# Moving the output stores and input loads of a cross-attention kernel to other steps of a tile

## What is computed

```python
q = heads(x @ W_q)
k_t, v_t = heads(text @ W_k), heads(text @ W_v)
probs_t = softmax(einsum('bhsd,bhtd->bhst', q, k_t) * attn_scale)
text_out = einsum('bhst,bhtd->bhsd', probs_t, v_t)
attn_scores = einsum('bhsd,bhnd->bhsn', q, k_ip) * attn_scale
qsem = l2norm(einsum('bhst,bte->bhse', probs_t, text))
fused = attn_scores + 0.5 * einsum('bhse,bne->bhsn', qsem, l2norm(ip))
probs_ip = softmax(fused) * spatial_mask
out = (text_out + probs_ip @ v_ip) @ W_out + b_out + x
```

## Time and profile before

| what | value |
|---|---|
| median of 3 runs | 1042.71 us (1041.78 to 1043.53) |
| time of the profiled execution | 1040.03 us |
| its span, first to last instruction | 1038.2 us |
| TensorE matmul busy | 981.1 us, 95% |
| VectorE / ScalarE / GpSimd busy | 78% / 68% / 62% |
| the DMA queue's packets, share of 16 engines | 84.3% |
| mean granted TensorE clock | 0.982 |

### The profile page before, as it was taken

The page is one execution under the profiler, slowest core; times in us unless marked ns, Lnnn a source line. Parts: engine busy times, 40 slices in busy tenths (PEclk is TensorE's granted clock), DMA queues, the critical chain, the costliest instruction groups (busy, mean ns, idle before and its releaser), DMA issues.

```text
span 1038.2 us, 24562 instructions
## 1 busy us (share of the span) xinstructions
PE 981.1 (95%) x7604; PEld 791.6 (76%) x7604; DVE 806.9 (78%) x2401; ACT 707.7 (68%) x2315; POOL 641.9 (62%) x1899
## 2 busy tenths in 40 slices
PE   7986778999999999999999999999999999999877
PEld 5755666888877888888877888888878888888755
DVE  4375678888978788888878888888868888887851
ACT  1354778777677777777766777777767787777720
POOL 1112467777676677667666767767756677676750
PEclk9988999999999999999999999999999999999989
DMA  9845988979799998888899989798889989679852
GB/s 292 325 129 133 192 160 157 165 169 186 160 191 178 186 190 172 172 169 169 156 200 180 186 172 182 156 187 167 164 179 193 177 172 184 138 158 150 161 116 74
DMA packets 483871, 180.26 MB, mean 174 GB/s; under 512 B 449517, under 2 KB 461855, under 8 KB 483740
## 3 DMA queue, kind: packets, MB, share of 16 engines
q1 hardware_dynamic: 483708, 178.62, 84.3%
q10 hardware_dynamic: 32, 0.07, 0.0%
HBM read 42.34 MB, written 27.22 MB: 67 GB/s over the span
## 4 chain that ended last, share of the span: by engine, by line
PE 76%; DMA 5%; DVE 3%; ACT 2%; SPq 2%; issue 2%; POOL 1%; POOLq 0%; DVEq 0%; ACTq 0%
PE ps_O L1149 25%; PE ps_Q L1183 25%; PE ps_S L1122 12%; PE ps_U L1169 11%; DMA pts<-ph 5%; PE ps_M L1199 3%; ACT pr L905 2%; SPq L825 1%; SPq L795 0%; ACT ph L917 0%; DVE smax L1014 0%; DVE pr L1060 0%; DVE n L1072 0%; SPq L785 0%; DVE bias L1021 0%
## 5 line engine op out<-in xcount | busy, mean ns | idle before, releaser
L905 ACT ACTIVATE pr<-ps_S,bias 128x73 f32<-128x73 f32 x1280 | 290.1, 339 | 130.4 <-DVE bias L1021 129.8
L987 POOL TENSOR_TENSOR ph<-pr,ph 128x220 f16<-128x220 f32 (+1 forms) x640 | 273.6, 460 | 153.4 <-ACT ph L917 153.3
L1149 PE MATMUL ps_O<-wo_hi,aT 128*128 128x320 f16 x1280 | 297.2, 303 | 5.6 <-DVE x_in L1006 3.5
L1183 PE MATMUL ps_Q<-xT,wq_hi 128*128 128x512 f32 x800 | 282.4, 418 | 6.8 <-DVE qT L994 6.5
L917 ACT ACTIVATE ph<-pr 128x292 f16<-128x292 f32 x640 | 234.2, 440 | 5.1
L1149 PE MATMUL ps_O<-wo_lo,aT 128*128 128x320 f16 x640 | 193.4, 302 | 0.0
L1169 PE MATMUL ps_U<-xm,pts 128*128 128x110 f16 (+1 forms) x2560 | 159.7, 213 | 20.6 <-DMA pts<-ph 17.6
L1149 PEld LDWEIGHTS ps_O<-wo_hi,aT 128*128 128x128 f16 x1280 | 126.0, 98 | 64.1 <-DVE x_in L1006 4.1
L1183 PEld LDWEIGHTS ps_Q<-xT,wq_hi 128*128 128x128 f32 x800 | 147.8, 193 | 34.8 <-DVE qT L994 8.1
L1169 PEld LDWEIGHTS ps_U<-xm,pts 128*128 128x128 f16 (+1 forms) x2560 | 144.6, 98 | 38.6 <-issue 14.5
L1122 PE MATMUL ps_S<-kbd,qT 128*128 128x308 f32 x960 | 168.5, 311 | 5.2 <-ACT pr L905 5.1
(11 more groups left out here) (185 smaller groups left out, 1273.2 us busy)
## 6 DMA issues: line engine op xcount, KB each, us to landing
out_dram<-x_in SPq DMA_DIRECT2D x64, 320.0 KB, 2.6
x_in<-in_x_dram SPq DMA_DIRECT2D x56, 320.0 KB, 3.2
pts<-ph SPq DMA_TRANSPOSE x320, 3.4
aT<-in_L_xattn_W_k_dram SPq DMA_DIRECT2D x5, 512.0 KB, 8.7
w_ip<-in_L_xattn_W_k_ip_dram SPq DMA_DIRECT2D x1, 2560.0 KB, 11.6
w_v<-in_L_xattn_W_v_dram SPq DMA_DIRECT2D x1, 2560.0 KB, 19.5
w_ip<-in_L_xattn_W_v_ip_dram SPq DMA_DIRECT2D x1, 2560.0 KB, 9.4
x_in<-in_x_dram SPq DMA_DIRECT2D x2, 1280.0 KB, 12.4
```

The lines of the kernel that those rows point to most:

```text
L905: last = nc.scalar.activation(pr[p % P_RING][:, j, h, :], sc[:, j, h, 0:T], ACT.Exp, bias=bias[p % 2][:, j, h:h + 1], scale=SCALE)
L987: nc.gpsimd.tensor_tensor(lo, full[:, :, t0:t1], one[:, :, 0, t0:t1], ALU.subtract).then_inc(pl_ready, 1)
L1149: last = nc.tensor.matmul(o_bank[half % 2][:, 0:HALF], stationary, moving, start=(k, a, b_) == O_MMS[0], stop=(k, a, b_) == O_MMS[-1])
L1183: last = nc.tensor.matmul(ps_Q[:], wq[a][:, c, k * P:(k + 1) * P], xT[(CC * i + c) % XT_RING][b_][:], start=(c, a, b_) == Q_MMS[0], stop=( ...
```

## The change

Two stores of a tile come one step later (from steps 5 and 7 to 6 and 8), and all four loads come one step later (from steps 1, 4, 6 and 8 to 2, 4, 7 and 9; the second one stays in step 4). The loop has one more step at its end, so that nothing is cut off. Nothing else changes; the number of DMAs and their sizes are the same.

```diff
-    FIRST, LAST = -4, STEPS * (TILES + 1) + 8
+    FIRST, LAST = -4, STEPS * (TILES + 1) + 9
...
-    STORE_AT = {10: 0, 13: 1, 15: 2, 17: 3}
-    LOAD_AT = (-19, -16, -14, -12)
+    STORE_AT = {10: 0, 13: 1, 16: 2, 18: 3}
+    LOAD_AT = (-18, -16, -13, -11)
```

## The result

| | before | after |
|---|---|---|
| median of 20 runs each | 1041.86 us (1038.34 to 1045.08) | 1044.53 us (1040.20 to 1049.07) |
| profiled execution, its span | 1040.03, 1038.2 us | 1049.07, 1047.3 us |
| mean granted TensorE clock | 0.982 | 0.980 |

The ratio is 1.0029, 95% interval 1.0016 to 1.0042: the change makes the kernel 2.7 us slower. The forecast was 2 us faster, and 1044.5 us lies outside its range.

A forecast was written before the change was run, and what follows sets the result against it. TensorE was taken to bound undisturbed tiles, SP's order to matter only in the switches and beginning. -0.65 - 0.3 - 0.9 - 1.0 + 0.8 = -2.05 us, from the median 1042.71 to 1040.7 us; range 1038.0 to 1044.2 us.

The forecast's parts named there:

- The undisturbed tiles: 0: Tiles with TensorE busy 55.00 of 55 us: later DMAs still land in time, so no time changes.
- The switches: Three switches, where TensorE waits for pts: moved stores let transposes issue earlier, -0.65, -0.3 and -0.9 us.
- rival 1: Switches: the moved load gives the gain back in full, switches 0, beginning -0.2, 1042.5 us; chance 20%.
- rival D: Switches, set up for the experiments: new pts waits behind them take back what the earlier ones gain; no chance given.
- The 0.7 and 0.4 us of slack: Transposes of steps 40 and 120: they land that much before TensorE needs them, leaving room for a gain.
- The third switch's clock: Behind the wait in step 118: granted clock of 0.55 for 3 us should stay at 1.00, worth some 1.3 us.
- Beginning, step 1: The load leaving step 1 frees the transposes TensorE awaits in step 3: 1.66 us go, 0.65 return, -1.0 us.
- Beginning, step 9: Tile 2's last load goes behind five vw DMAs, so TensorE waits 1.5 us for x: +0.8, bounds +0.4 and +2.5.
- rival 2: Switches and beginning: x rows land late and TensorE waits for them, slower, 1045.2 us; chance 8%.
- rival 3: Step 3's 2.70 us wait goes nearly whole and the third switch's clock stays up: 1038.0 us; chance 12%.

The follow-up runs named there:

- delay: A memset on GpSimd ahead of L961 in step 7, added to the kernel before (0.9994 of before) and to the change (1.0001).
- wait: GpSimd's L961 waits for the bias of its step, added to the kernel before (0.9962, 0.9930 of before) and to the change (0.9964, 0.9925).

## Why the prediction was wrong

**The step that failed first: "The undisturbed tiles: 0".** It looked only for a DMA that comes too late. In the profiled execution 11 of 13 tiles got longer all the same, by the 0.78 us of a held `bias`, a wait of TensorE for `qT` that the prediction did not have.

| trace | held of 13 | steps 0 to 9, 10 to 19, us |
|---|---|---|
| before, four | 0, 10, 1, 7 | 55.0, 52.2 on average |
| change, four | 11, 9, 9, 7 | 54.7, 54.4 on average |

On average 9.0 tiles against 4.5, times 0.78 us: +3.5 us. The counts alone don't prove that the change raises them, since those of before spread from 0 to 10. The timed runs support it. Taking the held tiles away gains 0.0006 (delay), 0.0038 and 0.0080 (wait; the second is 1.0010 less 0.9930) from the kernel before, 0.0041 on average where 4.5 held tiles would give 0.0034. From the change it gains 0.0038, 0.0065 (1.0029 less 0.9964, though on two chips) and 0.0092 (1.0017 less 0.9925), 0.0065 on average where 9.0 would give 0.0067. Each of the six carries 0.002 to 0.004, so it is their agreement that speaks. And without held tiles the two kernels are equal in three comparisons: 0.9962 and 0.9964, 0.9930 and 0.9925, 0.9994 and 1.0001. Each ratio carries about 0.002, so 1 to 2 us either way stay possible.

Why moved DMAs make this more frequent is open. In a trace, L961 of step 7 starts behind `bias` by a median of 0.053 us in the two traces of before with 0 and 1 held, and of 0.015 to 0.028 us in its other two and all four of the change. So the kernel before falls into either rhythm, and the change was seen in one only.

**The switches: the gain came back, and more.** The forecast had -0.65, -0.3 and -0.9. I sum what the steps take beyond their undisturbed length, held part taken out, as a mean over four traces each. Over the ten steps 34 to 43, 74 to 83 and 114 to 123 the three switches take 0.9, 0.6 and 0.1 us more than before. In steps 37 to 39, 77 to 79 and 117 to 119 the sum falls from 4.9 us to 1.1; in steps 40 to 43, 80 to 83 and 120 to 123 it grows from 4.4 us to 9.8. In the three traces each without held tiles the same two sums go from 5.0 to 4.6 and from 3.3 to 5.6.

The fall to 1.1 us is for the most part not the work of the moved DMAs. By trace the 4.9 us are 8.6 and 7.4 in the two traces of before with 0 and 1 held tiles, and 1.6 and 1.9 in the two with 10 and 7. In step 78 TensorE waits 2.03 and 2.00 us for `pts` in the first two, and 0 and 0.28 in the others, where the `bias` of step 77 is held: a held `bias` makes TensorE come later to a transpose that is late anyway. So in the switches the held part and the waits for `pts` overlap.

Switch 2 after the change shows how the gain comes back. TensorE's product in step 80 needs the transposes of step 78; SP in step 78, then TensorE, then the stretch behind, columns as in rows 1:

```profile
545.36 0.36 SPq L801 DMA_DIRECT2D out_dram<-x_in  x1
545.83 2.81 SPq L825 DMA_TRANSPOSE pts<-ph  x2
```
```profile
549.78 0.57 PE L1169 MATMUL ps_U<-xm,pts 128*128 128x110 f16 x8 [0.70 <-DMA pts<-ph]
551.22 0.58 PE L1169 MATMUL ps_U<-xm,pts 128*128 128x110 f16 x8 [0.88 <-DMA pts<-ph]
```
```profile
552.00:555.00 3.00, 3.00 (x10) 2.22 (x9) 1.95 (x6) 0.99 (x3) 2.65 (x7) 0.51 1.51 182
```

The 2.03 us of step 78 are gone, but step 80, with one wait of 0.69 us before, now waits 0.70 and 0.88, and 3.4 us at half clock follow. A store of the old price stands ahead of these transposes where a load stood, and the load of step 79 is behind them; SP is no faster (its transpose `aT` of step 77 took 2.94 us instead of 1.28), only TensorE comes earlier. This is rival 1's outcome, but not by the load in step 79 alone, and with a price that it did not have. Over four traces the waits in steps 40, 80 and 120 grow from 2.6 to 3.4 us, those in 42, 82 and 122, which are behind the moved load, from 0.5 to 2.7, and stretches of 3.4 us at half clock in steps 40 to 43, 80 to 83 and 120 to 123 from none to five. So rival D's mechanism exists. The 0.7 and 0.4 us of slack that I set against rival 1 were read from one trace, and for steps 42 and 122 only. The traces without held tiles have switches some 2 us longer with the change, while the timed runs without them show no difference, so its size is not pinned down.

**The third switch's clock: the number came, by luck in part.** The wait in step 118 is 0.23 us in the profiled execution, and the stretch behind it, at 0.55 before, runs at full clock:

```profile
767.00:770.00 3.00, 2.77 (x23) 2.26 (x20) 3.00 (x11) 2.40 (x10) 2.26 (x11) 1.00 1.02 225
```

But the `bias` of step 117 was held in this execution. The kernel before, in its trace with 7 held tiles, also waits only 0.39 us in step 118 and keeps its clock, while the change with the delayed GpSimd and no held tile there waits 1.30 and 0.27 and loses it. So the gain is not shown to be the moved store's. Step 120, without a wait before, now waits 1.26 + 0.25 us, and the half clock stands behind step 80 instead.

**Beginning, step 1: the term was half seen.** The 2.70 us in step 3 became 1.79 in this trace and 1.2 on average over four, near the 1 us forecast. But the 4.60 us of issue for two transposes is 5.16 us without any load ahead of it, so that price was not the load's. And step 4, with 0.69 + 0.35 us before, waits 3.40 us for transposes issued at 115.25, behind the load that moved here:

```profile
106.16 5.16 SPq L825 DMA_TRANSPOSE pts<-ph  x2
111.37 0.95 SPq L772 DMA_DIRECT2D x_d<-aT  x2
112.36 2.38 SPq L795 DMA_DIRECT2D xm<-x_d  x2
114.79 0.36 SPq L807 DMA_DIRECT2D x_in<-in_x_dram  x1
115.25 3.17 SPq L825 DMA_TRANSPOSE pts<-ph  x2
```
```profile
112.19 0.56 PE L1169 MATMUL ps_U<-xm,pts 128*128 128x110 f16 x8 [1.79 <-DMA pts<-ph]
...
119.84 1.39 PE L1169 MATMUL ps_U<-xm,pts 128*128 128x110 f16 x13 [3.40 <-DMA pts<-ph]
```

From 119 us on, still in this wait, the clock is at 0.54 for 7 us, near the level of 1.2 GHz. Over four traces steps 0 to 9 gain 0.35 us where 1.0 was forecast.

**Beginning, step 9: right in place, too small.** Steps 10 to 19 take 2.2 us more over four traces; +0.8 was forecast, +2.5 was its bound. The load goes out at 152.81 and TensorE waits 2.56 us, not 1.5 (2.14 and 0.45 us in two of the other traces; in the fourth the wait of step 10 is 1.89 us for `pts`):

```profile
149.89 2.88 SPq L853 DMA_DIRECT2D vw<-vw_d  x4
152.81 0.43 SPq L807 DMA_DIRECT2D x_in<-in_x_dram  x1
```
```profile
156.28 1.11 PE L1199 MATMUL ps_M<-ident,x_in 128*128 128x128 f32 x4 [2.56 <-DMA x_in<-in_x_dram]
```

The experiment on the last load alone puts this, with its waits in the switches, at 2 us. In the traces without held tiles steps 10 to 19 differ by 0.2 us only, since there the kernel before waits for `pts` in step 10 instead. The prediction's sign of rival 2, a wait for `x_in` at a switch, came in step 50:

```profile
383.43 0.66 PE L1199 MATMUL ps_M<-ident,x_in 128*128 128x128 f32 x4 [0.54 <-DMA x_in<-in_x_dram]
```

Steps 50 and 51 are 0.8 to 1.1 us longer in all four traces of the change; two name this wait (0.54 and 0.87 us), in the other two the transposes of `x` start some 0.3 us late without one. It lies behind the switch, in a tile that I had called undisturbed. So rival 2 was partly true, with waits of 2.56 and 0.54 us. That its 1045.2 us lie near the measured time is luck, since it had these waits at the switches and no held tiles. And rival 3's larger gain is seen nowhere in the times. The Trainium skill's rule to issue a DMA early and wait late (page "DMA: Bandwidth & Descriptors", section "Rules for kernel authors") is borne out by these two waits.

**A false sentence.** Of the loads, three move and the second stays in step 4. "Load q waits for a store that is then still more than ten steps old" is wrong. The store of tile j-4 comes one step ahead of the load of tile j: in steps 0, 3, 5, 7 against 1, 4, 6, 8, and now 0, 3, 6, 8 against 2, 4, 7, 9. It did no harm to the sum, since neither kernel puts both in one step. But it hid why stores and loads move together: the stores alone cost 11 us.

**The sum.** In the four traces: held tiles +3.5, the two groups of switch steps -3.8 and +5.4, steps 50 and 51 +0.9, beginning +1.8, elsewhere -1.4 (of which -1.2 ahead of step 0, where nothing was changed), together +6.4 us against spans of 1045.2 and 1038.9 on average. The timed medians say 2.7, and the profiled executions of the change lay 2.6 us above the medians of their kernels, those of before 1.1 below. So the sum is that of these traces; the shares, each uncertain by a microsecond or more, show the parts and not their exact prices.

## What to carry to other kernels

Before a DMA is moved past others in a saturated queue, look at the next transfer that the slot will delay, and at the buffer's own store: one step apart was enough here, the same step cost 1%. A wait that is taken away where the queue is saturated can come back two steps later, with the clock as a further price. Where VectorE and GpSimd start such a pair within 0.03 us of each other, treat that as a cost waiting to happen, and order the pair with a wait: 0.4 to 0.7% here, more than any move of a DMA gained. And take several traces of an unchanged kernel before a difference of 0.3% is explained by one.

## What the runs showed of the hardware

- **The edge is 0.03 us wide.** In the 130 tiles of ten traces (four of each kernel, stores only, loads 0 and 3 only), `bias` in step 7 is held in all 48 cases where L961 starts within 0.022 us behind it (and in three where L961 starts first), in none from 0.035 us on, and in either way between 0.024 and 0.030. Where a `memset` stands ahead of `bias` on VectorE it is held in 9 of 12 such cases. A held one takes up to 1.22 us, a free one mostly 0.17.
- **It repeats but is not fixed.** The same program had 0, 10, 1 and 7 held tiles in four executions.
- **Step 3 of each tile has the same meeting,** with `bias` at 1.0 to 1.2 us in 9 or more of 13 tiles of every trace without GpSimd's wait. It costs nothing there: step 3 takes 5.77 us with and without that wait. So a held instruction alone proves no loss; TensorE's row decides.
- **The clock.** Waits of 2.56 us here and 2.70 us were followed by 3 us near half clock, and one of 3.40 us went with 7 us of it. Two short waits, 0.70 and 0.88 us in step 80, were followed by 3 us as well, though TensorE worked between them; a wait of 2.03 us in step 78 before the change was followed by none.
